# Layer 1's tiles and the one-hots at multiples of 16 bytes, the adjacency in bands of eight groups

## The chip, the core and the metric

One core of a Trainium2 chip. The time is the device time of one execution in microseconds (us): 198.6 us, the median of 3 runs (198.57 to 199.79). TensorE is called PE in the profile (PEld is its load of the stationary operand), VectorE DVE, ScalarE ACT, GpSimd POOL, SyncE SP.

## The reference

Two message-passing layers on a graph of N = 3125 nodes with C = 64 features and E + N = 53125 directed edges sorted by target (25000 random pairs both ways, and a loop at every node). The layer adds a second loop with weight zero.

```python
def _mp_layer(x, src, dst, edge_attr, W, b):
    ...
    x_i = x[dst2]
    x_j = x[src2]
    msg = jnp.concatenate([x_i, x_j, ea2], axis=1) @ W + b
    agg = jax.ops.segment_sum(msg, dst2, num_segments=n)
    return jax.nn.relu(agg)
...
h = _mp_layer(x, src, dst, edge_attr, W1, b1)      # 64 -> 128
out = _mp_layer(h, src, dst, edge_attr, W2, b2)    # 128 -> 64
x = layernorm(x + log_softmax(out))
```

So per node one needs the sum of its neighbours' rows, its degree and the sum of its edges' weights; the rest is dense.

## The kernel before, in words

**Adjacency.** The nodes are cut into G = 25 groups of Q = 125. A window is five target nodes with up to 128 edges; there are 625 windows, 25 to a group, and they are taken in 79 sets of eight. For a set, VectorE compares keys with an iota in one instruction and so writes two one-hots per window (`onehots`, L513; the two are interleaved, so each is read in steps of 4 bytes, and a window's pair takes 500 bytes). TensorE multiplies the two one-hots of each window (`build`, L979) into one of two PSUM buffers `pset`, and ScalarE moves the result to `adj` in bf16 (`evacuate`, L818), group by group: a set that crosses from one group to the next takes two instructions. `adj` is laid out [group g][source group h][target e], so that block (g, h) is 125 contiguous elements and the next h lies 250 bytes on.

**Layer 1.** `layer1` (L989) adds adjacency block (g, h) as the stationary operand times tile h of x as the moving one, 195 columns: x in three bf16 parts of 65 columns (64 and a column of ones for the degree). Tile h begins 390 x h bytes into `x3`. `reduce_sums` (L541, VectorE) adds the three parts.

**Order.** Each engine runs its instructions in program order. TensorE's loop over b = 0 to 78 does `build(b + 4)`, then the eight layer-1 matmuls of set b, then what belongs to block b: keys of edge block j at `KEY_BLOCK[j]` (`turn_keys`), and the dense part of an epilogue of three groups at `TURN[i]` and the two blocks behind it (`turn_sums`, `hidden`, `messages`). ScalarE follows with `evacuate(b + 4)`, `distances(j)`, copies and casts. VectorE goes over the sets k with `onehots(k)` (three buffers, so it may be at most three sets ahead of the builds), and behind it `key_tiles`, `key_sums`, one of five `attr_sums` (L505, the sum of the edges' weights of block j, from `SUM_SET[j]` on), `reduce_sums`, `z_rest`, `z_low`. The edge sums go through two DMAs (SP's queue) and `split_sums` on GpSimd. The raw edges, keys and sums lie in the tail of `adj`, and the evictions that reach it wait until they are done with.

**Layer 2.** `layer2` (L1046) does the same with `z3` (tiles of 192 columns, 384 bytes apart) over all 625 blocks, behind layer 1. Six PSUM banks take turns: group g >= 6 waits at L1104 until the sum of group g - 6 has been read by VectorE. The first 21 source groups of groups 0 to 5 are done between the last two epilogues; their last four, and all else, wait for `z_low(last)`. VectorE adds the parts (L654) and goes through the final epilogue in six batches (`BATCHES`: 0-6, 6-12, 12-16, 16-19, 19-22, 22-25).

**`base_of`** (L620) is four dependent instructions on VectorE that finish what is added to a batch of layer-2 sums. It needs b2 and the last row of W2, both spread over the partitions in `b2w2`, and the edge sums. It is called for groups 0-12 and 12-16 behind the last `reduce_sums` and ahead of `z_rest(last - 1)` (L636 to L643), and for groups 16-25 in the first batch (L697). `b2w2` is loaded early (L1167, L1168).

Of the kernel before, what the change touches and what calls it, by code (L numbers as in the profile page):

```python
# [79 lines left out]
def gnn(nc, x, x_tiles, dst, edges, edge_attr, W1, b1, W2, b2, out, E):  # L80
# [3 lines left out]
    with ExitStack() as ctx:  # L84
# [24 lines left out]
        se = sb("se", [Q, G], FP32)  # L109
        se_rest = sb("se_rest", [Q, G, 2], FP32)  # L110
        stats_flat = sb("stats", [Q, VFROM + G * KB], BF16)
# [6 lines left out]
        still = adj[:, 4 * G * Q:4 * G * Q + 512]  # L118
        assert 4 * G >= (LEAD + 3) * SET

# [21 lines left out]
        off_idx = tail([Q, J], I32)  # L142
        sums_group = free[0] // (G * Q)
        pairs = tail([Q, J, 2 * SLOTS], I32)
# [20 lines left out]
        cnt2 = tail([Q, J], FP32)  # L165
        assert free[0] // (G * Q) > 5 and sums_group > 5 * (J - 1) + 2
# [6 lines left out]
        x3 = x3_flat[:, 0:G * XW].rearrange("p (g c) -> p g c", g=G)  # L173
        z3 = sb("z3", [Q, G, PW], BF16)
# [4 lines left out]
        turn = sb("turn", [128, EP * Q], FP32)  # L179
        turn_last = oh[1][:, :, :, :].rearrange("p a b c -> p (a b c)").bitcast(FP32)  # L180

# [7 lines left out]
        def late(shape):  # L189
# [22 lines left out]
        f_var = late([Q, BG])  # L212
        assert used[0] <= G * XW
        f_t = x3_flat[:, G * XW - 2 * 13 * C - 1:G * XW - 1].bitcast(FP32).rearrange("p (a b) -> p a b", a=13)

# [17 lines left out]
        gz_dram = nc.dram_tensor("gz_scratch", [N, C], FP32, kind="Internal").ap()  # L233
        deg_sum = sb("deg_sum", [Q, 1], FP32)
        ones_f = sb("ones_f", [Q, 1], FP32)
        flag = sb("flag", [1, 1], I32)
        free[0] = G * G * Q
# [100 lines left out]
        def _(gp):  # L338
# [15 lines left out]
            gp.tensor_copy(ident16[:, :], ident[:, 0:Q]).then_inc(consts, 1)  # L354
            gp.memset(ones_f[:, :], 1.0)
            gp.iota(iota2[:, :, :], [[1, SLOTS], [0, 2]], base=int(CODE), channel_multiplier=0,
# [29 lines left out]
            def split_sums(j):  # L386

                s0, s1, s2 = (stats[:, 5 * j:5 * j + 5, 3 + 3 * k:6 + 3 * k] for k in range(3))
                v = se[:, 5 * j:5 * j + 5]
                r = se_rest[:, 5 * j:5 * j + 5, :]  # L390
# [47 lines left out]
        def _(dve):  # L438
# [181 lines left out]
            def base_of(a, b):  # L620
# [6 lines left out]

                late_part = f_t[:, 0:b - a, :]
                dve.tensor_tensor(base[:, a:b, :], base[:, a:b, :], along(0), ALU.add)
# [14 lines left out]
            dve.tensor_reduce(deg_sum[:, :], stats[:, :, 0], AX.X, ALU.add).then_inc(deg_ready, 1)  # L644


            na = 0
            for i, (a, b) in enumerate(BATCHES):
# [49 lines left out]
                if i == 1:  # L698
                    dve.wait_ge(degs_ready, 1)
                    dve.tensor_scalar(flag[:, :], epb[0:1, 0, 0:1], float(E + N), None, ALU.not_equal)\  # L700
                       .then_inc(flag_ready, 1)
# [66 lines left out]
        def _(act):  # L768
# [49 lines left out]
            def evacuate(k):  # L818
                w, end = k * SET, k * SET + set_size(k)
                if w <= sums_group * G < end:  # L820

                    for j in range(J):
                        act.wait_ge(se_out[j], 16)
                if w <= 6 * G < end:
                    act.wait_ge(bw_in, 16 * 3 * EP)
                act.wait_ge(built, k + 1)
                rows = pset[k % 2][0:Q, :, :].rearrange("p b (w c) -> p (b w) c", c=128)
                while w < end:
                    g, i = divmod(w, G)
                    n = min(end - w, G - i)  # L830
                    ins = act.activation(adj4[0:Q, g, :, i * WD:(i + n) * WD].rearrange("p h (w e) -> p h w e", e=WD),  # L831
                                         rows[:, w - k * SET:w - k * SET + n, 0:WD * G].rearrange("p w (h e) -> p h w e", h=G),
                                         ACT.Copy)
                    w += n
                ins.then_inc(evac, 1)
# [42 lines left out]
            for b in range(NSETS):  # L878
# [74 lines left out]
        def _(pe):  # L953
# [196 lines left out]
        def _(sp):  # L1150
# [26 lines left out]
            with nc.allow_non_contiguous_dma(reason="one number per node"):  # L1177
                for j in range(J):
# [58 lines left out]
```

## Time and profile before

| | |
|---|---|
| Median of 3 runs | 198.6 us |
| Profiled execution | 199.66 us, its span 197.6 us |
| PE busy | 179.1 us (91%), 2051 matmuls |
| DVE busy | 166.2 us (84%) |
| ACT busy | 121.5 us (62%) |
| POOL busy | 38.1 us (19%) |
| Chain that ended last | PE 61%, DVE 19%, ACT 8%, DMA 7% |

The busy time of PE is modelled at its ends (a matmul's time includes its way through the array, 249 ns where the next starts after 87), so the pace is read from the starts or from the chain, not from the mean duration. The profiled execution is 0.5% longer than the median.

### The profile page before, as it was taken

How to read it: one execution, taken by the hardware profiler on the slowest of the kernel's cores; microseconds unless marked ns; L12 is line 12 of the kernel's file. 1: busy time of each engine (PE TensorE's matmuls, PEld its weight loads, DVE VectorE, ACT ScalarE, POOL GpSimd, SP SyncE). 2: the span in 40 equal slices, each digit the busy share in tenths (PEclk: the TensorE clock that was granted, in tenths of full speed). 3: DMA queues.
4: the chain of work that ended last, by engine and by line, in shares of the span. 5: the costliest groups of instructions: out<-in, count | busy, mean ns of one | idle time of the engine just before them, and what ended most of it. 6: DMA issues, size and time to landing. Idle time of an engine off the chain costs nothing.

```text
span 197.6 us, 5073 instructions
## 1 busy us (share of the span) xinstructions
PE 179.1 (91%) x2051; PEld 162.9 (82%) x2051; DVE 166.2 (84%) x395; ACT 121.5 (62%) x243; POOL 38.1 (19%) x57
## 2 busy tenths in 40 slices
PE   7678597999999999999899999999999999999940
PEld 2124487988889897989899999999999999999940
DVE  0889999999998999898999989926618978889773
ACT  2425896987888989999988999984220101021101
POOL 8488810000703423000701700000000000000000
PEclk9969999999999999999999999999999999999996
DMA  1335100000000000000000000000000010101010
GB/s 43 104 79 151 43 23 2 5 0 4 2 4 1 4 1 0 3 3 3 3 0 1 5 3 0 0 3 3 0 0 3 0 44 0 35 11 27 19 23 21
DMA packets 9031, 3.35 MB, mean 17 GB/s; under 512 B 8240, under 2 KB 8557, under 8 KB 9007
## 3 DMA queue, kind: packets, MB, share of 16 engines
q1 hardware_dynamic: 8207, 2.08, 4.9%
q0 software_dynamic: 800, 0.93, 2.0%
q8 instruction: 17, 0.28, 0.6%
q14 instruction: 7, 0.06, 0.1%
HBM read 2.18 MB, written 0.81 MB: 15 GB/s over the span
## 4 chain that ended last, share of the span: by engine, by line
PE 61%; DVE 19%; ACT 8%; DMA 7%; POOL 2%; issue 2%; ACTq 0%; DVEq 0%
PE pset L1049 18%; PE acc L1003 16%; DVE oh L518 12%; PE pset L985 10%; PE acc L1049 8%; ACT adj L831 4%; PE epb L1032 3%; PE epb L1043 3%; DMA adj<-in_edges,adj 3%; DMA adj<-in_dst 2%; DMA se<-se_scratch 2%; PE epb L1020 1%; ACT u L846 1%; DVE adj L527 1%; DVE x L532 1%
## 5 line engine op out<-in xcount | busy, mean ns | idle before, releaser
L518 DVE TENSOR_TENSOR oh<-iota,keys 128x2000 bf16<-128x2000 bf16 (+1 forms) x79 | 91.3, 1180 | 0.0
L831 ACT ACTIVATE adj<-pset 125x1000 bf16<-125x1000 f32 (+7 forms) x100 | 80.6, 840 | 9.6 <-PE pset L985 7.8
L1003 PE MATMUL acc<-x,adj 125*125 125x195 bf16 x625 | 66.5, 249 | 0.9 <-ACT adj L831 0.6
L1003 PEld LDWEIGHTS acc<-x,adj 125*125 125x125 bf16 x625 | 56.0, 137 | 1.5 <-ACT adj L831 0.8
L985 PE MATMUL pset<-oh 128*125 128x125 bf16 x625 | 51.1, 223 | 5.2 <-DVE oh L518 4.1
L985 PEld LDWEIGHTS pset<-oh 128*125 128x125 bf16 x625 | 45.0, 139 | 8.9 <-ACT adj L831 5.7
L1049 PE MATMUL pset<-z,adj 125*125 125x192 bf16 x425 | 36.8, 246 | 0.0
L1049 PEld LDWEIGHTS pset<-z,adj 125*125 125x125 bf16 x425 | 35.5, 136 | 0.1
L918 ACT ACTIVATE x<-x 125x192 f32<-125x192 f32 (+2 forms) x6 | 2.6, 428 | 32.4 <-DVE x L663 32.4
L1049 PE MATMUL acc<-z,adj 125*125 125x192 bf16 x200 | 17.5, 246 | 0.0
L393 POOL CAST stats<-se 125x15 bf16<-125x15 f32 x5 | 4.4, 881 | 66.7 <-DMA se<-se_scratch 66.7
L1049 PEld LDWEIGHTS acc<-z,adj 125*125 125x125 bf16 x200 | 16.8, 136 | 0.0
L547 DVE TENSOR_REDUCE u<-acc 125x65 f32<-125x195 f32 x25 | 8.9, 356 | 8.1 <-PE acc L1003 7.8
L957 PE MATMUL epb<-adj 128*128 128x512 bf16 x32 | 11.7, 521 | 1.2 <-DVE adj L447 1.2
L957 PEld LDWEIGHTS epb<-adj 128*128 128x128 bf16 x32 | 4.0, 127 | 6.5 <-issue 4.4
L654 DVE TENSOR_REDUCE x<-pset 125x64 f32<-125x192 f32 x17 | 5.4, 351 | 3.5 <-PE pset L1049 3.5
L370 POOL DMA_INDIRECT adj<-in_edges,adj x5 | 7.4, 1475 | 3.7 <-DVE adj L474 2.5
L374 POOL DMA_INDIRECT adj<-in_edge_attr,adj x5 | 7.7, 1549 | 1.5 <-issue 1.5
L1032 PE MATMUL epb<-turn,w1c 128*128 128x375 f32 x16 | 6.9, 512 | 0.5 <-ACT vt L855 0.4
L509 DVE SCALAR_TENSOR_TENSOR adj<-adj 125x128 bf16<-125x128 f32 x25 | 7.1, 282 | 0.0
L846 ACT ACTIVATE u<-x_nat,u 125x64 f32<-125x64 f32 x25 | 6.9, 343 | 0.0
L1043 PE MATMUL epb<-w2c,turn 128*125 128x128 f32 x48 | 6.7, 277 | 0.0
(122 smaller groups left out, 159.5 us busy)
## 6 DMA issues: line engine op xcount, KB each, us to landing
x_nat<-in_x_tiles SPq DMA_DIRECT2D x1, 406.2 KB
x_nat<-in_x_tiles SPq DMA_DIRECT2D x1, 375.0 KB
out<-x SPq DMA_DIRECT2D x2, 187.5 KB
out<-x SPq DMA_DIRECT2D x3, 93.8 KB
adj<-in_dst SPq DMA_DIRECT2D x1, 208.5 KB
bw<-adj SPq DMA_DIRECT2D x9, 1.0 KB
out<-x SPq DMA_DIRECT2D x1, 125.0 KB
adj<-in_edges,adj POOLq DMA_INDIRECT x5, 5.0
```

Source lines behind the costliest of these rows:

```text
L370: gp.indirect_dma_start(pairs[:, j, 0:2 * (SLOTS - LOOPS)], None, edges, bass.IndirectOffsetOnAxis(off_idx[:, j:j + 1], 0)).then_inc(pairs ...
L374: gp.indirect_dma_start(attrs[:, j, 0:SLOTS - LOOPS], None, edge_attr, bass.IndirectOffsetOnAxis(off_idx[:, j:j + 1], 0)).then_inc(attrs_i ...
L518: dve.tensor_tensor(out=oh[k % 3][:, 0:n, :, :], in0=iota2[:, 0:Q, :].unsqueeze(1).broadcast_to([128, n, Q, 2]), in1=keys[:, k * SET:k * S ...
L547: dve.tensor_reduce(u[i % 2][:, m, C:2 * C + 1], acc[g % 2][0:Q, 0:XW].rearrange("p (t c) -> p c t", t=3), AX.X, ALU.add)\
L831: ins = act.activation(adj4[0:Q, g, :, i * WD:(i + n) * WD].rearrange("p h (w e) -> p h w e", e=WD), rows[:, w - k * SET:w - k * SET + n, ...
L846: ins = act.activation(u[i % 2][:, m, 0:C], x_nat[:, a + m, :], ACT.Copy, scale=u[i % 2][:, m, 2 * C:2 * C + 1])
L957: pe.matmul(epb[:, 1, :], still[:, 0:128], still, start=True, stop=True)
L985: ins = pe.matmul(pset[k % 2][0:Q, i // 4, i % 4 * 128:i % 4 * 128 + WD * G], oh[k % 3][:, i, :, 0], oh[k % 3][:, i, :, 1], start=True, st ...
L1003: ins = pe.matmul(acc[g % 2][0:Q, 0:XW], adj4[0:Q, g, h, :], x3[:, h, :], start=(h == 0), stop=(h == G - 1))
L1032: pe.matmul(epb[:, 0, 0:n], w1c[:, :], flat(i)[:, 0:n], start=True, stop=False)
L1043: ins = pe.matmul(z_cols(b - a)[:, m, :], flat(i)[:, m * Q:(m + 1) * Q], w2c[:, :], start=True, stop=True)
L1049: ins = pe.matmul(bank2(g)[0:Q, :], adj4[0:Q, g, h, :], z3[:, h, :], start=(h == 0), stop=(h == G - 1))
```

## The change

- `x3` has tiles of 200 elements (400 bytes) of which 195 are used; `oh` has 256 elements (512 bytes) per window of which 250 are used; a build's moving operand is now the even elements, its stationary one the odd.
- `adj` is cut into bands of eight groups, [source group h][the band's targets] inside a band, so that an eviction of a set is always one instruction, and block (g, h + 1) lies 2000 bytes behind (g, h). The evictions wait for the scratch in `adj` at the first set of its band, set 50.
- For that, keys, distances and edge sums of blocks 3 and 4 come earlier (`KEY_BLOCK`, `DIST_BLOCK`, `SUM_SET`).
- For room, `b2w2` moves into `x3` and is loaded behind the last `reduce_sums`; the two calls of `base_of` move behind `z_low(last)`; small tensors are joined.

```diff
+XS = 200
-KEY_BLOCK = {1: 7, 2: 19, 3: 38, 4: 48}
-SUM_SET = {0: 16, 1: 24, 2: 31, 3: 45, 4: 54}
+KEY_BLOCK = {1: 7, 2: 19, 3: 34, 4: 45}
+DIST_BLOCK = {1: 2, 2: 14, 3: 28, 4: 34}
+SUM_SET = {0: 16, 1: 24, 2: 31, 3: 37, 4: 43}
+BAND = 8
+BANDS = tuple((a, min(a + BAND, G)) for a in range(0, G, BAND))
...
-        b2w2 = sb("b2w2", [Q, 2, C], FP32)
-        adj4 = adj[:, 0:G * G * Q].rearrange("p (g h e) -> p g h e", g=G, h=G)
+        bands = [adj[:, a * G * Q:b * G * Q].rearrange("p (h e) -> p h e", h=G) for a, b in BANDS]
...
-        keyl, keyr = keys[:, :, 0], keys[:, :, 1]
-        oh = [sb(f"oh{s}", [128, SET, Q, 2], BF16) for s in range(3)]
-        x3_flat = sb("x3", [Q, G * XW + 1], BF16)
+        keyr, keyl = keys[:, :, 0], keys[:, :, 1]
+        oh_flat = [sb(f"oh{s}", [128, SET, 256], BF16) for s in range(3)]
+        oh = [t[:, :, 0:2 * Q].rearrange("p w (q t) -> p w q t", t=2) for t in oh_flat]
+        x3_flat = sb("x3", [Q, G * XS], BF16)
+        b2w2 = late([Q, 2, C])
...
             def attr_sums(j, r0, r1):
                 dve.wait_ge(attrs_in[j], 16)
+                if j:
+                    dve.wait_ge(dist_ready, j)
...
             reduce_sums(G - 1)
+            z_rest(last - 1)
+            z_low(last - 1)
+            z_rest(last)
+            z_low(last)
             dve.wait_ge(b2_in, 16 * 2)
             for j in range(J):
                 dve.wait_ge(se_in[j], 16)
             base_of(0, BATCHES[1][1])
             base_of(BATCHES[1][1], BATCHES[2][1])
-            z_rest(last - 1)
-            z_low(last - 1)
-            z_rest(last)
-            z_low(last)
...
             def evacuate(k):
-                if w <= sums_group * G < end:
+                if w == scratch_band * BAND * G:
                     for j in range(J):
                         act.wait_ge(se_out[j], 16)
-                if w <= 6 * G < end:
                     act.wait_ge(bw_in, 16 * 3 * EP)
                 act.wait_ge(built, k + 1)
+                n = end - w
...
-                while w < end:
-                    g, i = divmod(w, G)
-                    n = min(end - w, G - i)
-                    ins = act.activation(adj4[0:Q, g, :, i * WD:(i + n) * WD]...
+                c = w // (BAND * G)
+                at_w = (w - c * BAND * G) * WD
+                ins = act.activation(bands[c][0:Q, :, at_w:at_w + n * WD]...
...
-                                    oh[k % 3][:, i, :, 0], oh[k % 3][:, i, :, 1], start=True, stop=True)
+                                    oh[k % 3][:, i, :, 1], oh[k % 3][:, i, :, 0], start=True, stop=True)
...
+            def block_of_adj(g, h):
+                return bands[g // BAND][0:Q, h, g % BAND * Q:(g % BAND + 1) * Q]
...
-                    ins = pe.matmul(acc[g % 2][0:Q, 0:XW], adj4[0:Q, g, h, :], x3[:, h, :],
+                    ins = pe.matmul(acc[g % 2][0:Q, 0:XW], block_of_adj(g, h), x3[:, h, 0:XW],
...
-            sp.dma_start(b2w2[:, 0, :], b2...).then_inc(b2_in, 16)
-            sp.dma_start(b2w2[:, 1, :], W2[2 * HID:2 * HID + 1, :]...).then_inc(b2_in, 16)
...
+            sp.wait_ge(acc_read, G)
+            sp.dma_start(b2w2[:, 0, :], b2...).then_inc(b2_in, 16)
+            sp.dma_start(b2w2[:, 1, :], W2[2 * HID:2 * HID + 1, :]...).then_inc(b2_in, 16)
```

## Rows read from the trace of the kernel before

**Rows 1.** Busy time by stage: us; busy of PE, PEld, DVE, ACT, POOL (x); PEclk, DMA, GB/s.

```profile
20.00:54.70 34.70, 29.88 (x369) 27.30 (x367) 34.50 (x59) 29.10 (x48) 8.94 (x8) 1.00 0.06 11
54.70:72.90 18.20, 18.18 (x220) 17.12 (x221) 17.53 (x34) 16.21 (x31) 4.02 (x6) 1.00 0.05 2
72.90:99.00 26.10, 24.95 (x305) 23.36 (x304) 24.30 (x49) 25.21 (x56) 6.38 (x10) 1.00 0.02 2
99.00:132.50 33.50, 33.50 (x422) 32.26 (x421) 29.43 (x43) 30.57 (x55) 4.28 (x5) 1.00 0.02 2
132.50:148.50 16.00, 16.00 (x185) 15.57 (x184) 7.53 (x16) 5.86 (x21) 0.00 (x0) 1.00 0.00 1
148.50:190.10 41.60, 41.56 (x503) 41.22 (x501) 34.73 (x140) 5.30 (x20) 0.00 (x0) 1.00 0.08 18
```

**Rows 2.** Chain of waits in order of time, 54 to 153 us: start, us, what.

```profile
54.72 0.51 PE epb L1020 x3
...
73.16 0.60 ACT adj L831
...
97.75 0.98 ACT adj L831 x2
...
111.00 0.49 PE pset L985 x8
111.49 0.69 PE acc L1003 x8
...
150.61 2.06 PE pset L1049 x25
```

**Rows 3.** Timeline of PE at 138.2 us: start us, us, engine line op.

```profile
138.24 0.33 PE L1034 MATMUL epb<-vt,bw 128*128 128x125 bf16 x3
138.40 0.41 PE L1049 MATMUL pset<-z,adj 125*125 125x192 bf16 x3
```

**Rows 4.** Groups by line and form: busy us, mean ns, idle before.

```profile
L831 ACT ACTIVATE adj<-pset 125x1000 bf16<-125x1000 f32 x57 | 57.5, 1021 | 7.7 <-PE pset L985 6.7
...
L509 DVE SCALAR_TENSOR_TENSOR adj<-adj 125x128 bf16<-125x128 f32 x25 | 7.1, 282 | 0.0
...
L831 ACT ACTIVATE adj<-pset 125x500 bf16<-125x500 f32 x6 | 3.3, 602 | 0.3 <-PE pset L985 0.2
```

**Rows 5.** DMA issues: KB each, median us to landing.

```profile
w2c<-in_W SPq DMA_DIRECT2D x2, 32.0 KB, 3.9
```

**Rows 6.** Timeline of DVE, 135 to 164 us.

```profile
135.95 0.96 DVE L629 TENSOR_TENSOR base<-base,b2w 125x768 f32<-125x768 f32 x1
...
141.05 0.42 DVE L632 TENSOR_TENSOR base<-base,x 125x256 f32<-125x256 f32 x1
...
147.99 0.19 DVE L644 TENSOR_REDUCE deg_sum<-stats 125x1 f32<-125x25 bf16 x1
149.00 1.35 DVE L654 TENSOR_REDUCE x<-pset 125x64 f32<-125x192 f32 x4 [0.81 <-PE pset L1049]
150.32 0.69 DVE L654 TENSOR_REDUCE x<-acc 125x64 f32<-125x192 f32 x2
...
160.38 1.15 DVE L654 TENSOR_REDUCE x<-pset 125x64 f32<-125x192 f32 x4
...
163.29 0.36 DVE L654 TENSOR_REDUCE x<-acc 125x64 f32<-125x192 f32 x1 [1.49 <-PE acc L1049]
```

**Rows 7.** Timeline of PE, 150 to 163 us.

```profile
150.45 2.23 PE L1049 MATMUL pset<-z,adj 125*125 125x192 bf16 x25
...
158.96 4.29 PE L1049 MATMUL acc<-z,adj 125*125 125x192 bf16 x50
```

**Rows 8.** Busy time around the early fall of the granted clock (PEclk).

```profile
6.25:9.66 3.41, 1.77 (x7) 0.73 (x7) 2.95 (x12) 1.68 (x4) 1.61 (x2) 1.00 0.44 140
9.66:13.07 3.41, 3.41 (x10) 1.22 (x9) 2.69 (x12) 1.48 (x3) 2.80 (x3) 0.50 0.31 70
13.07:16.50 3.43, 2.29 (x12) 0.94 (x10) 3.27 (x8) 1.34 (x4) 2.82 (x3) 1.00 0.47 118
```

More of the change, by code:

```diff
@@ L109, in gnn @@
         se = sb("se", [Q, G], FP32)
-        se_rest = sb("se_rest", [Q, G, 2], FP32)
+        se_rest = sb("se_rest", [Q, 5, 2], FP32)
         stats_flat = sb("stats", [Q, VFROM + G * KB], BF16)
@@ L115, in gnn @@
         adj = sb("adj", [128, G * G * Q + 1], BF16)
-        adj4 = adj[:, 0:G * G * Q].rearrange("p (g h e) -> p g h e", g=G, h=G)
-        still = adj[:, 4 * G * Q:4 * G * Q + 512]
-        assert 4 * G >= (LEAD + 3) * SET
+        bands = [adj[:, a * G * Q:b * G * Q].rearrange("p (h e) -> p h e", h=G) for a, b in BANDS]
+        assert BAND * G % SET == 0
+        still = adj[:, BAND * G * Q:BAND * G * Q + 512]
         free = [G * G * Q]
@@ L142, in gnn @@
         off_idx = tail([Q, J], I32)
-        sums_group = free[0] // (G * Q)
         pairs = tail([Q, J, 2 * SLOTS], I32)
@@ L165, in gnn @@
         cnt2 = tail([Q, J], FP32)
-        assert free[0] // (G * Q) > 5 and sums_group > 5 * (J - 1) + 2
+        scratch_band = free[0] // (G * Q) // BAND
+        assert scratch_band * BAND * G > (max(KEY_BLOCK[J - 1] + 4, SUM_SET[J - 1] + WD)) * SET
         keys = sb("keys", [128, WINDOWS, 2], BF16)
-        keyl, keyr = keys[:, :, 0], keys[:, :, 1]
-        oh = [sb(f"oh{s}", [128, SET, Q, 2], BF16) for s in range(3)]
-        x3_flat = sb("x3", [Q, G * XW + 1], BF16)
-        x3 = x3_flat[:, 0:G * XW].rearrange("p (g c) -> p g c", g=G)
+        keyr, keyl = keys[:, :, 0], keys[:, :, 1]
+        oh_flat = [sb(f"oh{s}", [128, SET, 256], BF16) for s in range(3)]
+        oh = [t[:, :, 0:2 * Q].rearrange("p w (q t) -> p w q t", t=2) for t in oh_flat]
+        x3_flat = sb("x3", [Q, G * XS], BF16)
+        x3 = x3_flat[:, :].rearrange("p (g c) -> p g c", g=G)
         z3 = sb("z3", [Q, G, PW], BF16)
@@ L179, in gnn @@
         turn = sb("turn", [128, EP * Q], FP32)
-        turn_last = oh[1][:, :, :, :].rearrange("p a b c -> p (a b c)").bitcast(FP32)
+        turn_last = oh_flat[1][:, :, :].rearrange("p a b -> p (a b)").bitcast(FP32)
         def flat(i):
@@ L212, in gnn @@
         f_var = late([Q, BG])
-        assert used[0] <= G * XW
-        f_t = x3_flat[:, G * XW - 2 * 13 * C - 1:G * XW - 1].bitcast(FP32).rearrange("p (a b) -> p a b", a=13)
+        assert used[0] <= G * XS
+        f_t = x3_flat[:, G * XS - 2 * 13 * C:G * XS].bitcast(FP32).rearrange("p (a b) -> p a b", a=13)
         pset = [pb(f"pset{s}", [128, 2, 512], FP32) for s in range(2)]
@@ L233, in gnn @@
         gz_dram = nc.dram_tensor("gz_scratch", [N, C], FP32, kind="Internal").ap()
-        deg_sum = sb("deg_sum", [Q, 1], FP32)
-        ones_f = sb("ones_f", [Q, 1], FP32)
-        flag = sb("flag", [1, 1], I32)
+        small = sb("small", [Q, 4], FP32)
+        deg_sum, ones_f, flag = small[:, 0:1], small[:, 1:2], small[0:1, 2:3].bitcast(I32)
         free[0] = G * G * Q
@@ L354, in _ @@
             gp.tensor_copy(ident16[:, :], ident[:, 0:Q]).then_inc(consts, 1)
-            gp.memset(ones_f[:, :], 1.0)
+            gp.memset(ones_f, 1.0)
             gp.iota(iota2[:, :, :], [[1, SLOTS], [0, 2]], base=int(CODE), channel_multiplier=0,
@@ L389, in split_sums @@
                 v = se[:, 5 * j:5 * j + 5]
-                r = se_rest[:, 5 * j:5 * j + 5, :]
+                r = se_rest
                 wide = [Q, 5, 3]
@@ L626, in along @@
                     return b2w2[:, k:k + 1, :].broadcast_to([Q, b - a, C])
-                late_part = f_t[:, 0:b - a, :]
+                late_part = f_t[:, 13 - (b - a):13, :]
                 dve.tensor_tensor(base[:, a:b, :], base[:, a:b, :], along(0), ALU.add)
@@ L639, in _ @@
             base_of(BATCHES[1][1], BATCHES[2][1])
-            z_rest(last - 1)
-            z_low(last - 1)
-            z_rest(last)
-            z_low(last)
-            dve.tensor_reduce(deg_sum[:, :], stats[:, :, 0], AX.X, ALU.add).then_inc(deg_ready, 1)
+            dve.tensor_reduce(deg_sum, stats[:, :, 0], AX.X, ALU.add).then_inc(deg_ready, 1)
             na = 0
@@ L699, in _ @@
                     dve.wait_ge(degs_ready, 1)
-                    dve.tensor_scalar(flag[:, :], epb[0:1, 0, 0:1], float(E + N), None, ALU.not_equal)\
+                    dve.tensor_scalar(flag, epb[0:1, 0, 0:1], float(E + N), None, ALU.not_equal)\
                        .then_inc(flag_ready, 1)
@@ L819, in evacuate @@
                 w, end = k * SET, k * SET + set_size(k)
-                if w <= sums_group * G < end:
+                if w == scratch_band * BAND * G:
                     for j in range(J):
                         act.wait_ge(se_out[j], 16)
-                if w <= 6 * G < end:
                     act.wait_ge(bw_in, 16 * 3 * EP)
                 act.wait_ge(built, k + 1)
+                n = end - w
                 rows = pset[k % 2][0:Q, :, :].rearrange("p b (w c) -> p (b w) c", c=128)
-                while w < end:
-                    g, i = divmod(w, G)
-                    n = min(end - w, G - i)
[L831 to L834, printed above, removed]
+                c = w // (BAND * G)
+                at_w = (w - c * BAND * G) * WD
+                ins = act.activation(bands[c][0:Q, :, at_w:at_w + n * WD].rearrange("p h (w e) -> p h w e", e=WD),
+                                     rows[:, 0:n, 0:WD * G].rearrange("p w (h e) -> p h w e", h=G), ACT.Copy)
                 ins.then_inc(evac, 1)
@@ L887, in _ @@
                 for j in range(1, J):
-                    if b == KEY_BLOCK[j] - 5:
+                    if b == DIST_BLOCK[j]:
                         distances(j)
@@ L1048, in layer2 @@
                 for h in range(h0, h1):
-                    ins = pe.matmul(bank2(g)[0:Q, :], adj4[0:Q, g, h, :], z3[:, h, :],
+                    ins = pe.matmul(bank2(g)[0:Q, :], block_of_adj(g, h), z3[:, h, :],
                                     start=(h == 0), stop=(h == G - 1))
@@ L1108, in _ @@
                     pe.wait_ge(rest_ready, last + 1)
-                    pe.matmul(epb[0:1, 0, 0:1], deg_sum[:, :], ones_f[:, :], start=True, stop=True).then_inc(degs_ready, 1)
+                    pe.matmul(epb[0:1, 0, 0:1], deg_sum, ones_f, start=True, stop=True).then_inc(degs_ready, 1)
             pe.wait_ge(flag_ready, 1)
@@ L1185, in _ @@
                       .then_inc(se_in[j], 16)
+            sp.wait_ge(acc_read, G)
+            sp.dma_start(b2w2[:, 0, :], b2.rearrange("(a n) -> a n", a=1).broadcast_to([Q, C])).then_inc(b2_in, 16)
+            sp.dma_start(b2w2[:, 1, :], W2[2 * HID:2 * HID + 1, :].broadcast_to([Q, C])).then_inc(b2_in, 16)
             for i, (a, b) in enumerate(BATCHES):
```

3 lines of the change are left out of this document (removed).

## Prediction

> **What bounds the kernel now.** I read the busy time by stage first, then the chain of waits, then the timelines of VectorE and TensorE around the two places where the chain could change hands. By stage [rows 1] there are four regimes. From 20.0 to 54.7 us VectorE is busy 34.50 of 34.70 us and TensorE 29.88: the one-hots set the pace, and faster matmuls only wait longer. From 54.7 to 132.5 the order on TensorE (a set of eight builds, then eight matmuls of layer 1) is the chain, broken by ScalarE: in 72.9 to 99.0 TensorE is idle 1.15 us and ScalarE busy 25.21 of 26.10, with evictions on the chain [rows 2]. From 132.5 to 148.5 TensorE is full and VectorE half idle. From 148.5 to 190.1 layer 2 fills TensorE (41.56 of 41.60). The last 7.5 us are the last batch's epilogue, which the change leaves alone.
>
> **Layer 1's moving operand.** x's tiles now begin every 390 bytes, afterwards every 400. Eight matmuls of layer 1 take 0.69 us, 86.3 ns each; 25 of layer 2, whose tiles lie 384 bytes apart, take 2.06, so 82.4 ns with 192 columns [rows 2]. Three more columns at 2.4 GHz are 1.2 ns, so 2.7 ns of each layer-1 matmul is what the start can be worth. From the point where TensorE takes the path over (54.72, layer 1 at set 22 of 79) 625 - 176 = 449 remain: 1.2 us.
>
> **The builds.** Their starts go from every 500 bytes to every 512, and the operands swap places. Eight take 0.49 us, 61 ns each [rows 2]; the three matmuls of 125 contiguous columns at 138.24 take 0.16 to the next start [rows 3], and 125 columns at 2.4 GHz with the 2.4 ns that layer 2's matmul has over its 80 are 54.5. So a build can gain at most 5.5 to 6 ns (all of the difference) and at least nothing (if the 4-byte step or the weight load makes it). I take 2.7, what the same cause is worth in layer 1. From set 26 on 625 - 208 = 417 remain: 1.1 us, ends 0 and 2.3.
>
> Both together are 2.3 us on TensorE, but where ScalarE leads the chain (three stretches between 73.16 and 98.8, 4.7 + 6.4 + 4.4 us, so about 15 of the 81 from 54.7 to 135.6; their first and last piece are in [rows 2]) they aren't on the path: 1.9 us.
>
> The Trainium skill, "Advanced Engine Details and Errata", SBUF Cachelines, tells of 16-byte lines with a penalty for a different line per access. Counted so, a build touches 32 lines wherever it starts, and a layer-1 tile 25 or 26: by that rule almost nothing is won, and the front would give 0.5 instead of 2.4. The 2.7 ns that the rows leave unexplained speak against it.
>
> **Evictions.** A set that crossed a group took two instructions, now one. 1000 elements take 1021 ns, two of 500 take 2 x 602 [rows 4]: 0.18 us less for 21 of 79 sets. Only where ScalarE leads is it on the path: some three such sets, 0.5 us; ends 0 and 1.5 (the idle of TensorE there, plus a little). The step between runs of five elements grows from 250 bytes to 2000; I cost it at nothing, since the time goes by elements.
>
> **Work moved in order.** The edge sums of blocks 3 and 4 (ten instructions of 0.28 us [rows 4], with their short reads), keys 3 and 4 and two pairs of distances come three to eleven sets earlier. The total is the same on VectorE and ScalarE. VectorE's idle time covers them: 0.67 us before 72.9 and 1.80 before 99.0 [rows 1]. That is thin: if it goes, up to 1 us of the front's gain goes with it, since the next one-hot is late. On ScalarE keys 3 now come beside an epilogue at block 34, and leave blocks 38 and 48 lighter. I take zero, between -1 and +0.8. The one wait that moves, the eviction of set 50 for the edge sums' stores, has three one-hots between the last sum and its build; I cost it at nothing. Front in all: 1.9 + 0.5 = 2.4 us, ends 0.5 and 4.5.
>
> **What is late next: `base_of`.** The two rows for it are loaded over x's tiles, after the last reduce of layer 1, by two loads on SP's queue. Nothing is queued there in front of them, and a load of this size takes 3.9 us to land [rows 5]: from 136 they are in by about 142. Its eight instructions on VectorE stand at 135.95 to 141.47 now, in idle time: 5.52 us [rows 6]. After the change they stand behind `z_low(last)`, whose end at about 148.0 is set by TensorE and ScalarE, not by VectorE. So they run from 148.0 to 153.5, with `deg_sum` behind them, and the first reduce of layer 2 starts at about 153.65 instead of 149.00 and ends 0.36 later. Queued behind them are all reduces, and TensorE waits for those: group 6 goes into group 0's bank. It starts at 150.45 now [rows 7] and at about 154.0 then: **3.5 us of standstill in the stage that TensorE bounds**. Later batches don't make it worse: VectorE's reduces 0 to 5 (2.01 us), the epilogue and the third `base_of` (9.37 from 151.01 to 160.38) and reduces 6 to 10 (1.42) end at about 166.5, and group 11 then ends at 163.25 + 3.5 = 166.8 [rows 6, 7]. From there both engines are shifted alike. Ends: 3.0 (if the eight instructions start before `z_low`'s end is out) and 4.0.
>
> **The clock in that standstill.** TensorE was granted 1.00 in 6.25 to 9.66 and was busy 1.77 of 3.41 us there; then the clock was 0.50, the lower level of 1.2 GHz, for 3.41 us; after 2.29 of 3.43 busy it had stayed at 1.00 [rows 8]. The new standstill is longer than the 1.64 us of idle time before that fall. So a fall is likelier than not. 3.41 us at half pace cost 1.7 if all of it is matmuls, and less where part of it is still the standstill: I take 1.2, ends 0 and 1.7. The Trainium skill, "TensorE: Matmul & The Clock Gate", under "Why this matters for your kernels", likewise warns of idle gaps between bursts of matmuls.
>
> **Sum.** -2.4 + 3.5 + 1.2 = +2.3 us. The profiled execution took 199.66 us with a span of 197.6, 2.06 outside it; that becomes a span of 199.9 and 202.0. It is 0.5% above the median of the runs, 198.6, so for the median I say **200.9**.
>
> **Rivals.**
> 1. No fall of the clock: all else as above, 198.6 - 2.4 + 3.5 = 199.7. For it: the standstill may lie so that the gate sees enough work around it. Against: rows 8.
> 2. Line counting holds, the starts win nothing: 198.6 - 0.5 + 3.5 + 1.2 = 202.8. The rule of the cachelines above is its ground; the 2.7 ns speak against.
> 3. `base_of` stays covered, the other side: its place is the first reduce of layer 2. If the eight instructions are through by 149.0, the standstill is gone and the front alone counts: 198.6 - 2.4 = 196.2. It decides from a standstill below 2.4 us. For it: VectorE is idle most of 141.5 to 149.0. Against: they stand in program order behind an instruction that ends at 148.0.
> 4. The front wins its upper end (builds at 55 ns, evictions off the chain) with the clock held: 198.6 - 4.5 + 3.5 = 197.6.
>
> **Chances.** Forecast 0.45, rival 1 0.25, rival 2 0.12, rival 3 0.10, rival 4 0.08. Range 197.0 to 202.8: down to rival 4 with half a us for its bounds, up to rival 2; it leaves out rival 3 and the upper half of rival 2. No change is within 1% (196.6 to 200.6), about what a measurement tells. Slower by over 1%: two thirds of the forecast (0.30), rival 2 and a little of rival 1: 0.44. Faster by over 1%: rival 3 with two thirds, and a part of rival 4 with a small standstill: 0.12. The rest, 0.44, is within.
>
> **What would show it.** Layer 1 at 83.6 ns a matmul and builds near 58, in groups of eight at 0.67 and 0.46 us. 79 evictions instead of 100. The last reduce of layer 1 about 2.4 us before 135.67. `base_of` directly behind `z_low(last)`, TensorE idle about 3.5 us before group 6 with a VectorE reduce as its releaser, and the granted clock at 0.50 behind it. The forecast is wrong if TensorE has no gap before group 6, or if the front gains more than 4.5 us.

## The result: slower by 2.4%

The changed kernel takes 204.16 us (median of 6 runs, 201.75 to 205.03) against 198.58 (6 runs); the ratio is 1.0237, 95% interval [1.0211, 1.0263]. The forecast was 200.9 with a range of 197.0 to 202.8: the sign and the place are right, the size is outside the range. The profiled execution took 205.03 us with a span of 203.0. The ratio leaves out the two longest of the six executions (204.80 and the profiled one) as slow; the two medians alone give 1.028, so the loss is 4.7 to 5.6 us, and the trace stands at the long end of it. Its busy time by stage, in the columns of [rows 1], with the stages cut at the same events:

```profile
20.00:54.40 34.40, 29.43 (x365) 26.88 (x364) 34.20 (x59) 27.94 (x40) 8.57 (x8) 1.00 0.05 11
54.40:72.60 18.20, 17.82 (x217) 16.69 (x218) 17.52 (x39) 16.07 (x30) 4.09 (x6) 1.00 0.05 3
72.60:98.30 25.70, 24.58 (x308) 23.24 (x307) 25.53 (x53) 24.23 (x49) 10.69 (x15) 1.00 0.04 2
98.30:131.30 33.00, 33.00 (x423) 31.92 (x423) 28.06 (x35) 29.75 (x49) 0.00 (x0) 1.00 0.01 2
131.30:147.10 15.80, 15.80 (x183) 15.34 (x182) 2.48 (x8) 5.76 (x21) 0.00 (x0) 1.00 0.02 5
147.10:152.80 5.70, 2.16 (x27) 1.97 (x24) 5.49 (x11) 0.00 (x0) 0.00 (x0) 0.87 0.01 3
152.80:195.00 42.20, 42.13 (x477) 41.68 (x477) 34.14 (x138) 5.30 (x20) 0.00 (x0) 0.94 0.08 17
195.00:203.00 8.00, 0.00 (x0) 0.00 (x0) 4.25 (x20) 0.98 (x4) 0.00 (x0) 0.76 0.09 20
```

What answers to [rows 1]: the stretch in which VectorE leads is as long as before, and VectorE is now also full in 72.6 to 98.3 (25.53 of 25.70). Layer 1 is through at about 134.3. New is the line 147.1 to 152.8: TensorE is busy 2.16 of 5.70 us and VectorE 5.49. Behind it the granted clock is 0.94 on average up to 195.0.

Five groups by form (busy us, mean ns, idle before), for [rows 4]:

```profile
L837 ACT ACTIVATE adj<-pset 125x1000 bf16<-125x1000 f32 x78 | 77.5, 1002 | 10.6 <-PE pset L989 9.4
L1011 PE MATMUL acc<-x,adj 125*125 125x195 bf16 x625 | 65.2, 248 | 0.8 <-ACT adj L837 0.5 <-DVE x L539 0.3
...
L989 PE MATMUL pset<-oh 128*125 128x125 bf16 x625 | 50.8, 222 | 5.6 <-DVE oh L525 4.5 <-ACT adj L837 1.0
L989 PEld LDWEIGHTS pset<-oh 128*125 128x125 bf16 x625 | 45.0, 139 | 9.0 <-ACT adj L837 5.6 <-DVE oh L525 1.4 <-issue 1.1
...
L1042 PEld LDWEIGHTS epb<-vt,bw 128*128 128x128 bf16 x25 | 2.1, 98 | 2.7 <-issue 1.7
```

79 evictions instead of 100, and 1002 ns for one of a full set: so the step of 2000 bytes instead of 250 costs nothing (1021 ns before). Then the pace, three lines of the chain of waits (start, us, what) for [rows 2]:

```profile
110.12 0.48 PE pset L989 x8
110.60 0.68 PE acc L1011 x8
...
134.28 0.32 PE epb L1028 x3
```

Eight matmuls of layer 1 take 0.68 instead of 0.69; from start to start they average 84.3 ns, before 86.6. Eight builds take 0.48, 60.7 ns each from the starts, before 60.9: the builds won nothing.

VectorE in the tail, for [rows 6]:

```profile
134.32 0.36 DVE L554 TENSOR_REDUCE u<-acc 125x65 f32<-125x195 f32 x1 [1.59 <-PE acc L1011]
140.25 0.36 DVE L562 TENSOR_TENSOR u<-epb,z 125x192 f32<-125x192 f32 x1 [5.57 <-ACT z L870]
...
146.50 0.23 DVE L569 TENSOR_TENSOR z<-u,z 125x64 bf16<-125x64 f32 x1 [0.32 <-ACT z L875]
146.78 0.96 DVE L636 TENSOR_TENSOR base<-base,x 125x768 f32<-125x768 f32 x1
...
151.88 0.43 DVE L639 TENSOR_TENSOR base<-base,x 125x256 f32<-125x256 f32 x1
152.34 0.20 DVE L651 TENSOR_REDUCE small<-stats 125x1 f32<-125x25 bf16 x1
152.45 1.14 DVE L661 TENSOR_REDUCE x<-pset 125x64 f32<-125x192 f32 x4
```

It waits 5.57 us for the epilogue where `base_of` used to run, and runs it from 146.78, directly behind `z_low(last)` at 146.50, to 152.31. The first reduce of layer 2 starts at 152.45. TensorE's wait for it, from the waits (who waits for whom: us, times, longest), then the two lines of the chain behind it, for [rows 7]:

```profile
PE pset L1057 <- DVE x L661: 3.6, 1, 3.6
```

```profile
152.85 4.26 PE pset L1057 x25
...
157.23 6.82 PE pset L1057 x75
```

The wait of 3.6 us is the standstill that was forecast. But group 6 then takes 4.26 us where 25 matmuls took 2.06. The granted clock says why (columns of [rows 8]):

```profile
149.00:151.37 2.37, 0.26 (x4) 0.07 (x1) 2.30 (x4) 0.00 (x0) 0.00 (x0) 1.00 0.00 0
151.37:158.19 6.82, 5.34 (x34) 5.08 (x35) 6.53 (x28) 0.73 (x2) 0.00 (x0) 0.50 0.00 0
158.19:161.00 2.81, 2.81 (x37) 2.81 (x36) 2.56 (x11) 0.41 (x2) 0.00 (x0) 1.00 0.00 0
```

TensorE was busy 0.26 of 2.37 us at the full clock; then the clock was 0.50 for 6.82 us, twice as long as after the early fall of [rows 8], and 5.34 us of that were matmuls. How long the clock stays low is not a property of the kernel: in a second trace of the kernel before (experiment 6) the early fall itself lasts 6.82 us.

```profile
7.36:14.18 6.82, 6.41 (x15) 2.38 (x16) 6.17 (x24) 2.74 (x5) 5.47 (x5) 0.50 0.38 104
```

**Where the time went.** Stretches between the same events in the profiled executions, worked out from the starts:

| us | before | changed |
|---|---|---|
| span's start to first one-hot | 15.97 | 15.71 |
| to layer 1 at set 22 | 39.64 | 39.64 |
| to the first matmul of layer 2 | 80.23 | 79.14 |
| to group 6 | 14.61 | 18.36 |
| to the last matmul | 39.37 | 41.89 |
| to the end of the span | 7.75 | 8.25 |

So -1.1 in the front, +3.75 standstill, +2.5 clock, +0.5 at the end, -0.3 at the start: +5.4 on the span. The first line varies by itself (15.09 to 15.97 in two traces of the kernel before), and the second by 0.3 (39.64 here, 39.36 in the trace of experiment 3, whose kernel is the same up to there). So parts are priced by the others, which repeat to 0.02 us in the kernel before. The +0.5 at the end lies wholly behind VectorE's last instruction: up to there from the last matmul it is 4.92 us in both, and then 3.33 us against 2.83. With it goes the last store; why it takes longer isn't shown.

### The profile page after: what moved, and what is told of

Same layout as the page of the kernel before. It is cut to its first block, busy times and chain, and to the rows that moved or that the text cites. A ratio compares the mean times of both kernels' runs of the same rounds, so it can differ in the third digit from the quotient of the medians.

```text
span 203.0 us, 5068 instructions
## 1 busy us (share of the span) xinstructions
PE 179.1 (88%) x2050; PEld 163.7 (81%) x2051; DVE 165.8 (82%) x395; ACT 118.6 (58%) x222; POOL 38.1 (19%) x57
## 4 chain that ended last, share of the span: by engine, by line
PE 57%; DVE 22%; ACT 7%; DMA 7%; issue 3%; POOL 2%; DVEq 0%; ACTq 0%
PE pset L1057 18%; PE acc L1011 14%; DVE oh L525 11%; PE pset L989 10%; PE acc L1057 7%; ACT adj L837 3%; PE epb L1040 3%; PE epb L1051 3%; DMA adj<-in_edges,adj 3%; DMA adj<-in_dst 2%; DMA se<-se_scratch 2%; ACT u L850 1%; PE epb L1028 1%; DVE adj L534 1%; DVE x L539 1%
## 5 line engine op out<-in xcount | busy, mean ns | idle before, releaser
L837 ACT ACTIVATE adj<-pset 125x1000 bf16<-125x1000 f32 (+1 forms) x79 | 77.7, 993 | 10.6 <-PE pset L989 9.4
L1011 PE MATMUL acc<-x,adj 125*125 125x195 bf16 x625 | 65.2, 248 | 0.8 <-ACT adj L837 0.5
L1011 PEld LDWEIGHTS acc<-x,adj 125*125 125x125 bf16 x625 | 54.8, 136 | 1.2 <-ACT adj L837 0.6
L989 PE MATMUL pset<-oh 128*125 128x125 bf16 x625 | 50.8, 222 | 5.6 <-DVE oh L525 4.5
L989 PEld LDWEIGHTS pset<-oh 128*125 128x125 bf16 x625 | 45.0, 139 | 9.0 <-ACT adj L837 5.6
L1057 PE MATMUL pset<-z,adj 125*125 125x192 bf16 x425 | 39.3, 255 | 3.6 <-DVE x L661 3.6
L1057 PEld LDWEIGHTS pset<-z,adj 125*125 125x125 bf16 x425 | 37.9, 143 | 3.8 <-DVE x L661 3.8
L398 POOL CAST stats<-se 125x15 bf16<-125x15 f32 x5 | 3.8, 758 | 49.8 <-DMA se<-se_scratch 49.8
L961 PE MATMUL epb<-adj 128*128 128x512 bf16 x31 | 10.2, 483 | 1.2 <-DVE adj L452 1.2
L562 DVE TENSOR_TENSOR u<-epb,z 125x192 f32<-125x192 f32 (+1 forms) x9 | 3.0, 339 | 9.5 <-ACT z L870 9.4
```

The costliest lines, as they stand in the source:

```text
L837: ins = act.activation(bands[c][0:Q, :, at_w:at_w + n * WD].rearrange("p h (w e) -> p h w e", e=WD), rows[:, 0:n, 0:WD * G].rearrange("p w ...
L961: pe.matmul(epb[:, 1, :], still[:, 0:128], still, start=True, stop=True)
L1011: ins = pe.matmul(acc[g % 2][0:Q, 0:XW], block_of_adj(g, h), x3[:, h, 0:XW], start=(h == 0), stop=(h == G - 1))
L1057: ins = pe.matmul(bank2(g)[0:Q, :], block_of_adj(g, h), z3[:, h, :], start=(h == 0), stop=(h == G - 1))
```

## Experiments

### 1. The deferral alone

The kernel before, with two blocks of lines exchanged:

```diff
-            dve.wait_ge(b2_in, 16 * 2)
-            ... se_in, base_of(0, 12), base_of(12, 16)
             z_rest(last - 1); z_low(last - 1); z_rest(last); z_low(last)
+            dve.wait_ge(b2_in, 16 * 2)
+            ... se_in, base_of(0, 12), base_of(12, 16)
```

> The kernel before with one edit: the two calls of base_of stand behind z_low(last), as in the changed kernel; b2w2 is still loaded early and all layouts are the old ones. Theory (the deferral is the loss): eight instructions of 5.5 us on VectorE start only at about 148.0, TensorE stands still about 3.5 us before group 6 and the granted clock falls to 0.50 behind it for up to 6.8 us, worth 2.8 us: 198.6 + 3.6 + 2.8 = about 205, with executions scattered over 202 to 206 by how long the clock stays low. Rival (the loss needs the new layout or the late load of b2w2): within 1 us of 198.6.

Measured 204.75 us, ratio 1.0294 [1.0251, 1.0338], executions from 202.57 to 205.34. Its chain of waits, and then its busy time after the standstill:

```profile
147.65 0.96 DVE base L629
...
153.40 0.28 DVE x L654
...
153.72 3.11 PE pset L1049 x25
```

```profile
155.00:158.40 3.40, 3.40 (x25) 3.14 (x23) 3.23 (x12) 0.53 (x1) 0.00 (x0) 0.50 0.00 0
```

The same picture without any new layout: `base_of` from 147.65, group 6 at 153.72, and it takes 3.11 us. The clock fell at 155.0 here, 1.3 us behind the start of group 6, was low for 3.4 us, and group 6 to the last matmul takes 40.97 us, 1.6 more than before. In the changed kernel it fell at 151.37, 1.5 us ahead of group 6, and cost 2.5. In both that is about half of the low time in which matmuls ran (3.4 and 5.34 us). The deferral alone loses as much as the change. That it loses a little more (all executions: 202.57 to 205.34 us against 201.75 to 205.03) would fit a change that wins something in front, but the difference is smaller than the spread of either and shows nothing.

### 2. The changed kernel with base_of covered

```diff
-        b2w2 = late([Q, 2, C])
+        b2w2 = iota2[0:Q]... .bitcast(FP32)         # 512 bytes, free after the last one-hot
...
-            z_rest(last - 1); z_low(last - 1); z_rest(last); z_low(last)
             ... base_of(0, 12), base_of(12, 16)
+            z_rest(last - 1); z_low(last - 1); z_rest(last); z_low(last)
...
-            sp.wait_ge(acc_read, G)
+            sp.wait_ge(oh_ready, NSETS)
             sp.dma_start(b2w2...)
```

> The changed kernel with base_of covered again: its two calls stand ahead of z_rest(last - 1) as in the kernel before, and b2w2 lies in the iota's tensor, which is free after the last one-hot, and is loaded then. Theory: no standstill before group 6, no fall of the clock there; what is left is the front's gain, 1.1 to 1.4 us: 197.3. Rival (the bands also cost something in layer 2 or in the evictions): 198.6 or more.

Measured 198.61 us, ratio 0.9991 [0.9970, 1.0012]. Busy time by stage:

```profile
147.10:149.30 2.20, 2.20 (x30) 2.20 (x29) 1.46 (x5) 0.00 (x0) 0.00 (x0) 1.00 0.02 7
149.30:188.90 39.60, 39.60 (x479) 39.26 (x477) 33.27 (x135) 5.30 (x20) 0.00 (x0) 1.00 0.08 18
```

No standstill, clock 1.00, TensorE full: 5.6 us are back. But not 197.3: the trace shows the front's -1.05 us and +0.34 at the end, and the ratio less still. By the number the rival is met (198.6 or more), but not by its cause in layer 2: the stretches to group 6 and to the last matmul are 14.61 and 39.37 us, as in the kernel before. Experiments 4 to 6 take this up.

### 3. The clock kept up through the standstill

```diff
+            for _ in range(15):
+                pe.matmul(epb[0:Q, 1, :], adj[0:Q, 0:Q], adj[0:Q, 0:512], start=True, stop=True)
             for g in range(6, G):
                 pe.wait_ge(acc2_read, g - 5)
```

> The changed kernel with 15 matmuls of 512 columns into a free PSUM bank ahead of TensorE's wait for group 0's reduce (3.2 us at full clock); the deferral itself stays. Theory (the standstill costs twice, by itself and by the clock): the standstill stays covered by idle work, the granted clock stays at 1.00, and 2.8 us come back: 198.6 - 1.3 + 3.6 = 200.9, the executions close together. Rival (the low clock behind the standstill isn't what makes the matmuls slow, or it falls anyway): 203.5 to 205.

Measured 202.02 us, ratio 1.0174 [1.0150, 1.0198], and the five executions lie within 0.7 us where the changed kernel's spread over 3.3. TensorE's timeline, then its busy time by stage:

```profile
147.85 0.82 PE L1058 MATMUL acc<-z,adj 125*125 125x192 bf16 x8
148.51 3.40 PE L1113 MATMUL epb<-adj 125*125 125x512 bf16 x15
152.26 0.96 PE L1058 MATMUL pset<-z,adj 125*125 125x192 bf16 x9 [0.35 <-DVE x L662]
```

```profile
148.50:152.20 3.70, 3.41 (x18) 1.93 (x15) 3.53 (x9) 0.00 (x0) 0.00 (x0) 1.00 0.00 0
152.20:156.30 4.10, 4.04 (x48) 3.89 (x49) 3.91 (x14) 0.52 (x1) 0.00 (x0) 1.00 0.00 0
156.30:160.00 3.70, 3.70 (x47) 3.70 (x46) 3.45 (x20) 0.62 (x3) 0.00 (x0) 1.00 0.00 0
```

The wait is as long (layer 2's start to group 6: 18.35 us), but 3.40 us of it are idle work, and the clock stays at 1.00. Group 6 to the last matmul takes 39.42 us instead of 41.89. Shown: the standstill costs 3.75, and what the clock does behind it another 2.5 in that trace. By the ratios, 1.0237 against 1.0174, it is 0.63%, 1.2 us, and by the medians of all executions, 204.16 against 202.02, 2.1 us: what a single trace lost to the clock is more than the kernel loses on average. So the theory holds in its cause, but 202.02 is 1.1 us above its 200.9. That the low clock's length is also what spreads the changed kernel's executions fits (the shortest had a mean granted clock of 0.979, the longest 0.965), but e_late_base's six do not line up so well (0.971 at 202.57, 0.975 at 204.56), so it is not shown.

### 4. x's tiles at 400 bytes, with and without the bands

The kernel before with `XS = 200` (and `se_rest` cut to make room):

> The kernel before with one edit: x's tiles lie 400 bytes apart instead of 390 (the scratch of the split sums is cut to make room). Theory: 84.3 ns for a layer-1 matmul instead of 86.6, 449 of them behind 54.7 us, so 1.0 us less: 197.6. Rival (the gain is taken back by ScalarE where it leads): 198.3 to 198.6.

Measured 198.82 us, ratio 1.0001 [0.9986, 1.0016]. Layer 1's pace is 84.4 ns, as said; but from set 22 to layer 2 it takes 79.83 us instead of 80.23: 0.40 of the 1.0. The theory's 197.6 is missed, the rival (ScalarE takes it back) is nearer. And experiment 2 with `XS = 195`:

> e_covered with x's tiles at 390 bytes again: bands, early sums and one-hots at 512 bytes stay. Theory (bands and the 400-byte tiles each give part of the 1.1 us): layer 1 at 86.6 ns, the stretch from set 22 to layer 2 about 0.6 us longer than in e_covered (79.8 against 79.18), so 199.2. Rival (VectorE and ScalarE, not the matmuls, set the front's end): the stretch stays at 79.2.

Measured 198.37 us, ratio 0.9999 [0.9984, 1.0014]; the stretch is 79.69 us against 79.18, near the theory's 79.8, though the time isn't its 199.2. So the tiles are worth 0.4 to 0.5 us here too, not 1.2. What the matmuls win, TensorE partly waits for again: in the stretch the 449 matmuls of layer 1 take 0.96 us less in e_x400's trace than before, and the waits behind them 0.38 us more (1.80 against 1.42).

### 5. The one-hots alone, and the order alone

The kernel before with 512 bytes a window and the operands swapped:

> The kernel before with the one-hots' part alone: 512 bytes a window, operands swapped. Theory (a build's start is worth nothing, its pace is set by the step or the load): builds at 60.8 ns, layer 1 at 86.6, 198.6 within 0.4 us. Rival (the recorded forecast's 2.7 ns a build): 197.5.

Measured 198.79 us, ratio 1.0000 [0.9982, 1.0018]; builds at 60.8 ns, the stretch 80.13 us. The theory holds.

The kernel before with `KEY_BLOCK`, `DIST_BLOCK` and `SUM_SET` of the changed one:

> The kernel before with the order alone: keys, distances and edge sums of blocks 3 and 4 at the changed kernel's places. Theory (VectorE's cover is thin: the moved sums delay set 36 by 0.6 us and what is lost comes back by set 50): 198.6, between 198.3 and 199.0, with set 36 late in the trace. Rival (it stays lost): 199.2 or more.

Measured 199.58 us, ratio 1.0044 [1.0022, 1.0066]: slower, on the rival's side (199.2 or more: it stays lost). The stretch takes 80.58 us, 0.35 more, and the end 8.09, 0.33 more. One wait of TensorE is new in it and in the changed kernel (who waits for whom):

```profile
PE epb L1023 <- ACT keys L806: 0.6, 1, 0.6
```

Keys 3 are now copied by ScalarE at block 34, behind the two instructions of `distances(4)` and beside an epilogue, and `turn_sums(2)` at block 35 waits for them. It is not the only change. TensorE's timeline, first of this kernel, then of the kernel before, has:

```profile
67.50 0.90 PE L1035 MATMUL epb<-turn,w1c 128*128 128x375 f32 x2 [0.47 <-ACT vt L858]
```

```profile
68.11 0.84 PE L1032 MATMUL epb<-turn,w1c 128*128 128x375 f32 x2
...
77.84 0.90 PE L1032 MATMUL epb<-turn,w1c 128*128 128x375 f32 x2 [0.41 <-ACT vt L855]
```

The epilogue at block 29 did not wait before and now waits 0.47 us for ScalarE, which has `distances(3)` of block 28 in front of its copies; the one at block 35 waited 0.41 us before and now has the keys' wait in its place. Two waits of 0.47 and 0.59 stand where one of 0.41 was. That these make the 0.35 us is argued from the order; each alone was not tried. At the end VectorE has a gap in front of its last instruction (its timeline):

```profile
193.46 0.16 DVE L693 SCALAR_TENSOR_TENSOR x<-x 125x3 f32<-125x3 f32 x1
193.90 0.36 DVE L696 TENSOR_TENSOR x<-x 125x192 f32<-125x192 f32 x1 [0.27 <-DVE x L693]
```

0.27 us of idle time that no semaphore explains. It stands in the traces of eight of the ten kernels with the moved sums (not in the changed kernel's own nor in the filler's, the two whose TensorE stands before group 6), and in none of the six without them. The time behind VectorE's last instruction is longer too with the moved sums: 2.85 to 3.45 us in the ten, 2.80 to 2.85 in the six. The cause of both stays open.

By difference, and if the parts add up, which no run shows, the bands with their whole evictions are then worth 0.8 to 0.9 us: -1.09 + 0.40 + 0.10 - 0.35 = -0.94, or from 79.69 against 80.23, -0.54 + 0.10 - 0.35 = -0.79.

### 6. The kernel before once more

> The kernel before, unchanged, for a second trace and for the spread of the measurement: the first profiled execution took 199.66 us where the median is 198.6. All theories: 198.5 us, ratio 1.000. If the difference of 1.1 us is in the wait for a DMA or in the clock of the first 30 us, the stages from 54.7 us on are as long as in the first trace; if it is spread over them, the front's price has to be taken against this trace.

Measured 198.38 us, ratio 0.9987 [0.9969, 1.0006]: 0.2% is what two equal kernels can differ by here. Its span is 196.7 us, 0.9 shorter than in the first trace, and all of that lies ahead of the first one-hot (15.09 against 15.97 us); all later stretches are equal to 0.02 us. The first trace was one with a slow start, not with a slow front.

### 7. What holds a build

Four kernels on top of experiment 2 change what the builds read. They do not compute the right adjacency, only the pace of a build counts, and each ran once:

```diff
-    pset[..][0:Q, ..], oh[k % 3][:, i, :, 1],      oh[k % 3][:, i, :, 0]
+    pset[..][0:Q, ..], oh[k % 3][:, i, :, 1],      oh_flat[k % 3][:, i, 0:Q]   # e_mov_contig
+    pset[..][0:Q, ..], oh_flat[k % 3][:, i, 0:Q],  oh[k % 3][:, i, :, 0]       # e_stat_contig
+    pset[..][0:Q, ..], oh_flat[k % 3][:, i, 0:Q],  oh_flat[k % 3][:, i, 0:Q]   # e_both_contig
+    pset[..][:, ..],   oh_flat[k % 3][:, i, 0:128], oh_flat[k % 3][:, i, 0:Q]  # e_contig_w128
```

> e_covered with a build's moving operand read as 125 contiguous elements at a multiple of 16 bytes instead of every second one (so the adjacency is not the right one; the flag that calls the repair path is held at zero). Only the pace of a build counts. Theory A (the 4-byte step of the moving operand holds a build at 61 ns): 55 ns a build, eight in 0.44 us. Theory B (the load of the stationary operand with its 4-byte step holds it): 60 to 61 ns as before.

> The same with the stationary operand contiguous and the moving one in steps of 4 bytes (the adjacency is again not the right one). Theory A: 60 to 61 ns. Theory B: 55 ns.

> Both operands contiguous, read from the same 125 elements (the adjacency is not the right one). Theories A and B: 55 ns a build. Theory C (something else, such as the load of 125 stationary columns at all, holds a build): 58 ns or more here too.

> e_both_contig with 128 stationary columns (the adjacency is not the right one). Theory C: 55 ns a build. Rival (PSUM or something else holds a build at 58.6): 58 to 59 ns.

Eight builds in the chain of waits of each, in this order:

```profile
110.12 0.48 PE pset L989 x8
```

```profile
109.33 0.47 PE pset L989 x8
```

```profile
109.82 0.47 PE pset L989 x8
```

```profile
109.50 0.44 PE pset L989 x8
```

From the starts: 60.2, 59.4, 58.6 and 55.1 ns; the four executions took 198.63, 197.54, 198.60 and 196.50 us. Theories A and B both fall: neither step alone holds a build, together they are worth about 2 ns, and the missing 3.5 come with 128 stationary columns instead of 125. That is theory C, which the groups after the change already hint at: a load of 125 columns takes 139 ns (L989), one of 128 takes 98 (L1042). The load's time goes with the columns and not with the step: 140 ns in e_both_contig, 97 in e_contig_w128.

### 8. 128 stationary columns in the whole computation

```diff
+            for t in oh_flat:
+                gp.memset(t[:, :, 2 * Q:256], 0.0)
...
-    ins = pe.matmul(pset[k % 2][0:Q, ..], oh[k % 3][:, i, :, 1], oh[k % 3][:, i, :, 0], ...)
+    ins = pe.matmul(pset[k % 2][:, ..], oh_flat[k % 3][:, i, 1:256:2], oh[k % 3][:, i, :, 0], ...)
```

> e_covered with 128 stationary columns per build instead of 125 (three columns of a cleared pad, still in steps of 4 bytes; the result is the same). Theory C (the load of the stationary operand is slower at 125 columns than at 128: loads take 139 ns in a build and 98 ns at L1034, where 128 columns are loaded and the pace is 55): a build at 55 to 57 ns, loads near 98 ns, up to 2 us less than e_covered on TensorE, so 197 to 198. Rival (the 4-byte step holds it): 60 to 61 ns and 198.6.

Measured 197.59 us, ratio 0.9961 [0.9948, 0.9974]: faster than both kernels, by 0.4% against the kernel before, beyond the 0.2% of experiment 6. Two groups by form, and eight builds in its chain:

```profile
L991 PE MATMUL pset<-oh 128*128 128x125 bf16 x625 | 49.5, 221 | 3.6 <-DVE oh L527 2.0 <-ACT adj L839 1.5
L991 PEld LDWEIGHTS pset<-oh 128*128 128x128 bf16 x625 | 40.8, 98 | 7.0 <-ACT adj L839 4.0 <-issue 2.5
```

```profile
110.04 0.46 PE pset L991 x8
```

Loads at 98 ns, builds at 58.1 ns with the 4-byte steps still in them, between theory C's 55 to 57 and the rival's 60 to 61; the stretch to layer 2 is 78.59 us, against 79.18 in experiment 2. On the kernel before, without bands, moved sums or 400-byte tiles:

> The kernel before with one-hots at 512 bytes and 128 stationary columns per build; no bands, no moved sums, x's tiles at 390 bytes. Theory C: builds at 55 to 57 ns, about 1.5 us less between 54.7 us and layer 2, 197.4. Rival (the 4-byte step holds a build): 198.6.

Measured 197.92 us, ratio 0.9976 [0.9966, 0.9985]; builds at 58.3 ns, the stretch 79.67, 0.56 us less than before and not the 1.5 of the theory. Against e_oh512 (80.13) three columns more save 0.46 us. By the times, of the padding only this use of it pays by itself, and barely more than the 0.2% by which equal kernels differ. The steps are the 3 ns between 58.1 and 55.1; a one-hot layout without them that computes the right adjacency was not tried.

## Why the prediction was wrong in size

The mechanism of the forecast came true. Two terms of its sum were mis-sized: the front's gain (-2.4, measured -1.1) and the cost of the low clock (+1.2, measured +2.5 in the trace and 1.2 to 2.1 by the executions); a third, the end, had none (+0.5 in the trace). Experiment 3 shows that the clock alone doesn't account for the miss: with the clock held, the forecast's terms give rival 1's 199.7, and that kernel took 202.02. Of these 2.3 us its trace has 1.3 in the front, 0.25 in the standstill and 0.3 at the end.

**The deferral of base_of: right.** Place, releaser and order as written: 5.5 us behind `z_low(last)`, first reduce at 152.45, TensorE waiting 3.6 us, 3.75 in the ledger against 3.5 forecast. Later batches added nothing: in the filler's trace group 6 to the last matmul is as long as before (39.42 against 39.37).

**The clock: right that it falls, wrong in how long.** The step "3.41 us at half pace ... I take 1.2, ends 0 and 1.7" took the one low stretch of the trace as the length of every one. The changed kernel's was 6.82 us and cost 2.5; e_late_base's was 3.4 and cost 1.6; and the kernel before had one of each length at its start, 3.41 and 6.82 us in its two traces. The upper end of 1.7 was too low. It is a term that varies by execution, so the range had to be wide to the slow side.

**Layer 1's tiles: pace right, worth wrong.** 2.7 ns were forecast and 2.3 measured, and the start is the cause: in the kernel before the matmuls whose tile begins at a multiple of 16 bytes (h = 0, 8, 16, 24) already took 83.6 to 84.0 ns from start to start and all others 86.6 to 88.0; after the change all take 83.9 to 84.6. "1.2 us", less a fifth for ScalarE, should have been 0.4: what is won is given back at the waits for ScalarE and VectorE, whose work per set did not shrink. That the share of the chain on TensorE was four fifths doesn't tell how much faster it can run before the next engine is there.

**The builds: wrong.** "I take 2.7, what the same cause is worth in layer 1" carried a price from one reading pattern to another: it was 0.1 to 0.2 ns. A build is held by its load of 125 columns and by the steps, the two causes that the prediction named for its lower end of nothing. The Trainium skill, "Advanced Engine Details and Errata", section SBUF Cachelines, tells of 16-byte lines and of a penalty where each access falls into another line. Counted by lines as in the prediction, a build touches 32 wherever it starts, so nothing is won, and the builds' 60.9 and 60.7 ns agree. For layer 1 the same count gives 25 or 26 lines, so hardly a gain, and there the traces disagree, with 2.3 ns. On the load the Trainium skill, "TensorE: Matmul & The Clock Gate", section Weight-path perf modes, says that a fast weight load is on with 128 weights of a type other than FP32. The runs agree: the builds' load took 98 ns with 128 columns and 139 with 125.

**Evictions: too low.** 0.5 us forecast, 0.8 to 0.9 by difference, under the assumption that the parts add up; within the ends.

**The moved work: wrong.** "I take zero" between -1 and +0.8; it costs 0.35 us in front and 0.33 at the end, and 0.4% measured by itself. The named risk was VectorE's cover, and VectorE did fill up (25.53 of 25.70 us), but the new waits of TensorE are for ScalarE: its copy of keys 3, and its copies behind `distances(3)`.

Front in all: -1.1 instead of -2.4; clock +2.5 instead of +1.2; end +0.5 not priced. The three errors have the same sign, which is why a forecast with the right mechanism left its range. Of the sums worked out beforehand, Rival 2's (no gain by the starts, 202.8) was the closest, by luck: its cause holds for the builds but not for layer 1's matmuls, and it has the clock's cost as low as the forecast. What stays open is why the ratios of e_covered and e_covered_x390 (0.9991, 0.9999) show less than their traces' -0.7 and 0.3 us. A resolution of 0.2% hides most of it, and e_covered_x390's trace alone has 0.6 of its +0.85 us at the end behind VectorE's last instruction (3.45 us against 2.83), a time that no run tells to be typical.

## What to carry to other kernels

Before an instruction is deferred "out of the way", find the next thing that waits behind it on its engine: idle time ahead of a gated instruction is cover, time behind it may be none. Price a standstill of TensorE twice, once by its length and once by the low clock behind it, and allow that clock several microseconds: here it was low for 3.4 us in one trace and 6.8 in another. A shorter matmul is worth only what the engines that feed and drain it can follow: here 0.4 of 1.2 us.

## What was not expected of the hardware

- A load of 128 stationary bf16 columns took 97 to 98 ns and one of 125 took 136 to 140; with 125-column matmuls behind them the pace was 55.1 against 58.6 ns (both operands contiguous), and 58.1 against 60.8 (4-byte steps). With three columns of padding a build was faster than with none.
- A moving operand of 195 contiguous bf16 columns ran at about 84 ns from a multiple of 16 bytes and at about 87 from the other starts (86.6 to 88.0 in the kernel before). In steps of 4 bytes the start made hardly a difference (60.9 and 60.7 ns).
- The low clock behind a standstill of 3.6 us lasted 3.4 us in one kernel's trace and 6.82 in another's with the same wait, and the early low stretch lasted 3.41 and 6.82 us in two traces of one kernel; 15 idle matmuls in the standstill kept the clock at 1.00.
